# Square rows of three batches as two float32r products, one unit later, with VectorE's order refitted

## The chip, the cores and the metric

The kernel runs on 1 core of one Trainium2 chip. The metric is the device time of one execution in microseconds (us). Several runs are taken and the median is used. The engines are TensorE (PE, with its weight loads as PEld), VectorE (DVE), ScalarE (ACT), GpSimd (POOL) and SyncE (SP, which here only issues DMAs).

## What is computed

The inputs are x (4 batches of 256 channels by 512 nodes), ctx_4096 (4 batches of 1601 point dimensions by 512 nodes) and fside (4 blocks of 256 by 256 weights). Each batch has 512 nodes. Its 8 nearest neighbours are those with the smallest squared distance between columns of the points, the node itself included. Two rounds of the same four blocks follow, with one matrix for the centre and the neighbours:

```python
sq = jnp.sum(xyz * xyz, axis=1)
d2 = sq[:, :, None] + sq[:, None, :] - 2.0 * jnp.einsum('bdn,bdm->bnm', xyz, xyz)
_, idx = jax.lax.top_k(-d2, k)
...
for i in range(NUM_BLOCKS):
    shortcut = points
    p = _lrelu(points)
    g = _group_point(p, idx_t)
    c = jnp.einsum('oi,bin->bon', w_center[i], p)
    gn = jnp.einsum('oi,bikn->bokn', w_neighbor[i], g)
    points = (c + gn.sum(axis=2)) / (K + 1.0) + shortcut
```

xyz is ctx_4096, points is x, and both weights are fside. The order of distances decides the result, so the Gram products and the rest must keep float32 precision.

## The kernel before

**Products in parts.** A float32 operand is split into float32r parts: high, low and a mixed sum of both. Main products (high with high, low with low) and mixed products together give the full product. In this way TensorE works with float32r throughout. The exceptions are the square row, which is a plain float32 product, and the transposes.

**Gram stages.** For each batch b from 0 to 3, the 1601 point dimensions come in 7 units k: six of 256 dimensions and a rest of 65. For a unit, SyncE loads `raw`. ScalarE makes `g_high` (`points_high`, L522). `g_low` comes from VectorE (`points_low`, L656). For the units 1, 3 and 5 of batches 1 to 3 it comes from ScalarE, as minus high (L539), and then a GpSimd DMA that adds the source to it (L288). VectorE makes `g_mixed` (`points_mixed`, L670). TensorE does `main_products` (16 products for a unit) and `mixed_products` (8). SyncE reloads `raw` of unit k for the next batch only when TensorE has used the unit and VectorE has made its `g_mixed` (L231). All of this has in-order queues written out by hand, one list for each engine, with semaphores between them.

**Distances, one batch behind.** While TensorE does the products of batch b, the distances of batch b-1 are made. VectorE folds the two sums into `gram` (`gram_rows`, L707) and takes the diagonal, times -0.5, into `half_diag`, and its row sums into `half_sq` (`diagonals`, L716). TensorE multiplies all ones by `half_diag` (`square_row`, L377), which puts minus half the square of each column in every row of a PSUM bank. VectorE adds it up (`distances`, L723). TensorE turns the blocks that were left out (`turn_distances`, L388) and ScalarE copies them (`copy_low`, L548). VectorE finds the 8 largest of each row and marks them (`neighbours`, L731), ScalarE makes `nbr` of the marks (L557), VectorE adds the diagonal (`add_selves`, L740), SyncE turns them by DMA (`turn_neighbours`, L245) and ScalarE copies the result into `adj` (`copy_adj`, L565).

**Steps.** The 32 steps (8 layers of 4 batches) run after the Gram stages; the first enters in stage 3. For step s, ScalarE makes relu and `r_high` (L576), GpSimd `r_low` (L295), VectorE `r_mixed` (L685). TensorE makes y (`y_main`, L400, and `y_mixed`, L423). ScalarE rounds it to `y_hi` (L595). VectorE takes the rest `y_rest` (L745) and with the mixed product makes `y_lo` (L753). TensorE multiplies both by the adjacency (`out_step`, L437) in two halves, and VectorE adds them to the state (`update`, L761). In TensorE's list, `y_mixed(s)` stands between the two halves of `out_step(s - 1)`. Step 0 differs: its y_mixed stands ahead of `square_row(3)` and of the first half of `out_step(0)`.

**Lines that set the order around the change.** TensorE's list is in L457 to L515, ScalarE's in L601 to L652, VectorE's in L768 to L827 and GpSimd's in L304 to L317. In stages 1 to 3 the square row stands behind mixed_products(b, 0) in TensorE's list, at L465. In VectorE's list `distances(b - 1)` stands at L784, between low 2 and mixed 2.

Of the kernel before, what the change touches and what calls it, by code (L numbers as in the profile page):

```python
# [25 lines left out]
def knn_blocks_kernel(nc: bass.Bass, x: bass.AP, ctx_4096: bass.AP, fside: bass.AP, out: bass.AP):  # L26
# [41 lines left out]
    with es:  # L68
# [31 lines left out]
        half_diag = sb("half_diag", [P, N], fp32)  # L100
        half_sq = sb("half_sq", [P, NB], fp32)
# [97 lines left out]
        diag_ready = sem("diag_ready")  # L199
        sq_row_ready = sem("sq_row_ready")  # L200
# [86 lines left out]
        def _(pool):  # L287
# [6 lines left out]

            def relu_low(n):  # L295

                if n == 0:
                    pool.wait_ge(unit_used, (B - 1) * PAIRS + 2)
                for h in range(CH):
                    pool.wait_ge(r_high_ready, CH * n + h + 1)  # L300
                    nc.gpsimd.tensor_tensor(r_low[:, n % 3, h, :], relu[:, h, :], r_high[:, n % 3, h, :].bitcast(fp32),  # L301
                                            ALU.subtract).then_inc(r_low_ready, 1)
# [10 lines left out]
            for b in range(1, B):  # L313
                for k in BY_DMA:
                    points_low(b, k)
# [4 lines left out]
        def _(pe):  # L320
# [56 lines left out]
            def square_row(b):  # L377
# [3 lines left out]
                else:  # L381
                    pe.wait_ge(w_high_ready, BLOCKS)
                    pe.wait_ge(w_rest_ready, BLOCKS)
                pe.wait_ge(diag_ready, b * NB + NB)
                nc.tensor.matmul(bank[SQ_BANK][:, :], ones[:, :], half_diag[:, :], start=True, stop=True)\  # L385
                    .then_inc(sq_row_ready, 1)
# [70 lines left out]
            for b in range(B):  # L457
# [4 lines left out]
                else:  # L462
                    main_products(b, 1)
                    mixed_products(b, 0)
                    square_row(b - 1)  # L465
                main_products(b, 2)
                mixed_products(b, 1)
                if b > 0:
                    turn_distances(b - 1)
                main_products(b, 3)  # L470
# [47 lines left out]
        def _(act):  # L518
# [13 lines left out]

            def points_parts(b, k):

                points_high(b, k)
                if by_dma(b, k):
# [63 lines left out]

            for k in range(UNITS):  # L601
# [11 lines left out]
            for b in range(1, B):  # L613
                points_parts(b, 5)
                points_parts(b, 6)
                copy_low(b - 1)
                if b >= 2:
                    copy_adj(b - 2)
                if b == 1:
# [20 lines left out]
            for s in range(1, B * LAYERS):  # L640
# [3 lines left out]
                if s == 1:  # L644
                    copy_low(B - 1)
                    copy_adj(B - 2)
# [8 lines left out]
        def _(dve):  # L655
# [60 lines left out]
            def diagonals(b):  # L716

                for n, i in enumerate(ROWS):
# [57 lines left out]
            for b in range(1, B):  # L776
# [7 lines left out]
                distances(b - 1)  # L784
                points_mixed(b, 2)
                points_low(b, 3)
                points_low(b, 4)
                points_mixed(b, 3)
                points_low(b, 5)
                neighbours(b - 1, 0)  # L790
                neighbours(b - 1, 1)
                points_low(b, 6)
                points_mixed(b, 6)
                points_mixed(b, 4)
                neighbours(b - 1, 2)
# [12 lines left out]
            diagonals(B - 1)  # L808
            relu_mixed(1)
            y_low(0)  # L810
# [42 lines left out]
```

## Time and profile before

| what | value |
|---|---|
| time, median of 3 runs | 321.87 us (321.72 to 322.04) |
| time of the profiled execution | 321.73 us |
| its span | 319.9 us |
| TensorE busy | 314.8 us, 98% |
| VectorE busy | 251.7 us, 79% |
| ScalarE busy | 172.6 us, 54% |
| GpSimd busy | 94.0 us, 29% |
| stage 1, stage 2, stage 3 begin | 29.9, 54.4, 78.9 us |

Times in the trace count from the start of the span. The page gives each engine's busy time. The chain that ended last is followed back from the last instruction: at each step to what released it, or to the instruction before it on its engine. A timeline row gives the start, the length, the engine, the line, the operation and what it writes and reads; in square brackets stand the idle time of the engine ahead of it and what ended that. A record's length includes the time in which it waits for a port, and matmul records overlap, so TensorE's pace is read from starts or from the chain.

### The profile page before, as it was taken

The page shows a single profiled execution, that of the slowest core. Times are in us where ns is not written, and L with a number is a line of the kernel's source. Part 1 is how long each engine was busy: PE and PEld are TensorE (multiplying, and loading weights), DVE is VectorE, ACT ScalarE, POOL GpSimd, SP SyncE. Part 2 cuts the span into 40 slices and gives each one's busy share as a digit, 9 for nine tenths or more (in the row PEclk, how much of TensorE's full clock was granted, in tenths as well). Part 3 has the DMA queues.
Part 4 walks back from the last instruction along what each step waited for, and adds up shares of the span by engine and source line. Part 5 has one row for each costly group of instructions (what it writes and reads, how often), then busy time and mean ns, then how long its engine had stood idle before and what let it go on. Part 6 is the DMA issues. An engine that isn't in the chain of part 4 may idle for free.

```text
span 319.9 us, 5033 instructions
## 1 busy us (share of the span) xinstructions
PE 314.8 (98%) x1974; PEld 287.5 (90%) x1974; DVE 251.7 (79%) x333; ACT 172.6 (54%) x255; POOL 94.0 (29%) x85
## 2 busy tenths in 40 slices
PE   8999999999999899999999999999999999999996
PEld 6999999999999688898888988888888988889885
DVE  3995799899899969998777767777776767767674
ACT  4557387388377346546584455444554455544530
POOL 2011111101126304433344333443344333443330
PEclk9999999999999999999999999999999999999999
DMA  7979959988950300000300000000000000000113
GB/s 251 315 284 198 267 166 223 237 283 190 261 92 1 66 2 0 2 0 2 66 1 2 1 3 0 0 0 2 0 2 0 2 0 0 2 0 2 67 67 134
DMA packets 17313, 25.52 MB, mean 80 GB/s; under 512 B 9476, under 2 KB 10756, under 8 KB 17288
## 3 DMA queue, kind: packets, MB, share of 16 engines
q1 hardware_dynamic: 15992, 20.46, 21.3%
q0 software_dynamic: 1296, 4.72, 8.2%
q8 instruction: 16, 0.26, 0.3%
q14 instruction: 9, 0.07, 0.1%
HBM read 20.98 MB, written 2.10 MB: 72 GB/s over the span
## 4 chain that ended last, share of the span: by engine, by line
PE 96%; DVE 2%; DMA 1%; issue 0%; ACT 0%; DVEq 0%
PE wide L444 38%; PE wide L323 29%; PE wide L417 18%; PE wide L433 9%; DMA raw<-in_ctx_dram 1%; PE wide L385 1%; PE wide L392 1%; PE wide L373 1%; DVE gram L713 0%; DVE y_lo L757 0%; DVE r_mixed L690 0%; PE wide L396 0%; DVE half_diag L720 0%; ACT g_high L527 0%; DVE state L765 0%
## 5 line engine op out<-in xcount | busy, mean ns | idle before, releaser
L301 POOL TENSOR_TENSOR r_low<-relu,r_high 128x512 fp32r<-128x512 f32 x64 | 83.7, 1331 | 135.7 <-ACT r_high L593 135.7
L444 PE MATMUL wide<-adj,y_hi 128*128 128x512 f32 (+1 forms) x260 | 101.8, 393 | 1.2 <-DVE y_lo L757 1.2
L444 PE MATMUL wide<-adj,y_lo 128*128 128x512 f32 (+1 forms) x260 | 101.7, 393 | 0.0
L598 ACT CAST y_hi<-wide 128x1024 fp32r<-128x1024 f32 x32 | 32.6, 1018 | 89.2 <-PE wide L417 89.2
L750 DVE TENSOR_TENSOR y_rest<-wide,y_hi 128x1024 f32<-128x1024 f32 x32 | 39.1, 1223 | 30.3 <-ACT y_hi L598 30.2
L765 DVE SCALAR_TENSOR_TENSOR state<-wide,state 128x512 f32<-128x512 f32 (+1 forms) x65 | 44.1, 678 | 20.0 <-PE wide L444 19.9
L444 PEld LDWEIGHTS wide<-adj,y_hi 128*128 128x128 f32 x260 | 49.0, 188 | 10.7 <-issue 2.0
L444 PEld LDWEIGHTS wide<-adj,y_lo 128*128 128x128 f32 x260 | 48.9, 188 | 8.7
L593 ACT ACTIVATE r_high<-relu 128x512 fp32r<-128x512 f32 x64 | 40.6, 634 | 2.0
L590 ACT ACTIVATE relu<-state 128x512 f32<-128x512 f32 x64 | 40.2, 627 | 1.5 <-POOL r_low L301 1.5
L757 DVE SCALAR_TENSOR_TENSOR y_lo<-wide,y_rest 128x1024 fp32r<-128x1024 f32 x32 | 39.1, 1222 | 0.0
L690 DVE SCALAR_TENSOR_TENSOR r_mixed<-r_low,r_high 128x1024 fp32r<-128x1024 f32 x32 | 38.9, 1216 | 0.2 <-POOL r_low L301 0.2
L433 PEld LDWEIGHTS wide<-w_mixed,r_mixed 128*128 128x128 f32 x256 | 34.5, 188 | 2.9
L417 PEld LDWEIGHTS wide<-w_high,r_high 128*128 128x128 f32 x256 | 34.6, 188 | 2.6
L417 PE MATMUL wide<-w_low,r_low 128*128 128x256 f32 x256 | 35.5, 281 | 0.0
L417 PE MATMUL wide<-w_high,r_high 128*128 128x256 f32 x256 | 35.4, 280 | 0.0
L433 PE MATMUL wide<-w_mixed,r_mixed 128*128 128x256 f32 x256 | 35.3, 280 | 0.0
L323 PE MATMUL wide<-g_high 128*128 128x256 f32 x192 | 34.4, 322 | 0.3 <-ACT g_high L527 0.3
L530 ACT ACTIVATE g_high<-raw 128x1024 fp32r<-128x1024 f32 x23 | 23.9, 1064 | 17.5 <-DMA raw<-in_ctx_dram 17.5
L417 PEld LDWEIGHTS wide<-w_low,r_low 128*128 128x128 f32 x256 | 32.4, 188 | 0.2 <-POOL r_low L301 0.2
L323 PE MATMUL wide<-g_low 128*128 128x256 f32 x192 | 32.2, 310 | 0.0
L323 PE MATMUL wide<-g_mixed 128*128 128x256 f32 x192 | 31.5, 310 | 0.0
(57 smaller groups left out, 285.7 us busy)
## 6 DMA issues: line engine op xcount, KB each, us to landing
raw<-in_ctx_dram SPq DMA_DIRECT2D x23, 512.0 KB, 5.5
g_low<-in_ctx_dram POOLq DMA_DIRECT2D x9, 512.0 KB, 7.9
state<-in_x_dram SPq DMA_DIRECT2D x4, 512.0 KB, 8.9
out_dram<-state SPq DMA_DIRECT2D x3, 512.0 KB, 2.8
w_raw<-in_fside_BxSxS_dram SPq DMA_DIRECT2D x1, 1024.0 KB, 7.8
rest_raw<-in_ctx_dram SPq DMA_DIRECT2D x4, 130.0 KB
raw<-in_ctx_dram SPq DMA_DIRECT2D x2, 256.0 KB, 3.2
turned<-nbr SPq DMA_TRANSPOSE x16, 3.1
```

The costliest lines, as they stand in the source:

```text
L301: nc.gpsimd.tensor_tensor(r_low[:, n % 3, h, :], relu[:, h, :], r_high[:, n % 3, h, :].bitcast(fp32), ALU.subtract).then_inc(r_low_ready, 1)
L323: return nc.tensor.matmul(sums_of(i, first), part[t][:, i * P:(i + 1) * P], row_of(i, part[t]), start=(start and i < NB - 1), stop=(stop a ...
L417: mm = nc.tensor.matmul(wide[main_at(s)][:, q * C:(q + 1) * C], part[:, s % 3, h, q * P:(q + 1) * P], weights[:, w, h, :], start=(part is ...
L433: mm = nc.tensor.matmul(dst, r_mixed[:, s % 3, h, q * P:(q + 1) * P], w_mixed[:, w, h, :], start=(h == 0), stop=(h == CH - 1))
L444: mm = nc.tensor.matmul(bank[to][:, cols], part[:, s % 2, q, h * P:(h + 1) * P], adj[:, b, q, cols], start=(q == 0 and part is y_hi), stop ...
L590: nc.scalar.activation(relu[:, h, :], state[:, b, h, :], ACT.Prelu, alpha=SLOPE)\
L593: nc.scalar.mul(r_high[:, n % 3, h, :], relu[:, h, :], LEAN).then_inc(r_high_ready, 1)
L598: nc.scalar.copy(y_hi[:, s % 2, :, :], wide[main_at(s)][:, :].rearrange("p (q o) -> p q o", q=NB))\
L690: nc.vector.scalar_tensor_tensor(r_mixed[:, n % 3, :, :], r_low[:, n % 3, :, :].bitcast(fp32), -SHIFT, r_high[:, n % 3, :, :].bitcast(fp32 ...
L750: nc.vector.tensor_tensor(y_rest[:, :, :], wide[main_at(s)][:, :].rearrange("p (q o) -> p q o", q=NB), y_hi[:, s % 2, :, :].bitcast(fp32), ...
L757: nc.vector.scalar_tensor_tensor(y_lo[:, s % 2, :, :], wide[MIXED][:, :].rearrange("p (q o) -> p q o", q=NB), UNMIX, y_rest[:, :, :], op0= ...
L765: nc.vector.scalar_tensor_tensor(state[:, b, h, cols], bank[at][:, cols], SHARE, state[:, b, h, cols], op0=ALU.mult, op1=ALU.add).then_inc ...
```

## The change

The square rows of batches 0 to 2 are made of two float32r products in place of one float32 product. ScalarE rounds `half_diag` to float32r (`diag_high`), GpSimd subtracts it from `half_diag` (`diag_low`), and TensorE sums ones times each in the same bank. Batch 3's square row stays as it was. `diag_high` stands in ScalarE's list behind `points_high(b, 5)`, and `diag_low` in GpSimd's list ahead of the DMA of unit 5. TensorE's square row stands one unit later, behind `main_products(b, 2)`, and `turn_distances` behind `main_products(b, 3)`. In VectorE's list `distances` moves behind mixed 3, and low 4 and mixed 3 move ahead of it; neighbours 0 and 1 move behind the rest and mixed 4. ScalarE does `copy_adj` ahead of `copy_low`. For step 0, VectorE makes `y_lo` ahead of `r_mixed` of step 1. New waits guard the reuse of half_diag, diag_high and diag_low.

```diff
--- before.py
+++ after.py
@@ -98,6 +98,10 @@
         dist = sb("dist", [P, NB, N], fp32)
         marked = sb("marked", [P, NB, N], fp32)
         half_diag = sb("half_diag", [P, N], fp32)
+
+        diag_high = sb("diag_high", [P, N], fp32r)
+        diag_low = sb("diag_low", [P, N], fp32r)
+        ones_r = sb("ones_r", [P, P], fp32r)
         half_sq = sb("half_sq", [P, NB], fp32)
         top8 = sb("top8", [P, NB, K], fp32)
         nbr = sb("nbr", [P, NB * (N + P)], bf16)
@@ -197,6 +201,9 @@
         main_copied = sem("main_copied")
         gram_ready = sem("gram_ready")
         diag_ready = sem("diag_ready")
+        diag_high_ready = sem("diag_high_ready")
+        diag_low_ready = sem("diag_low_ready")
+        ones_r_ready = sem("ones_r_ready")
         sq_row_ready = sem("sq_row_ready")
         dist_ready = sem("dist_ready")
         low_turned = sem("low_turned")
@@ -292,6 +299,14 @@
                 pool.dma_start(g_low[k][:, :, :], src[:, 2 * k:2 * k + 2, :], accum_op=ALU.add)\
                     .then_inc(low_landed[k], 16)
 
+            def diagonal_low(b):
+
+                pool.wait_ge(diag_high_ready, b + 1)
+                if b > 0:
+                    pool.wait_ge(sq_row_ready, b)
+                nc.gpsimd.tensor_tensor(diag_low[:, :], half_diag[:, :], diag_high[:, :].bitcast(fp32), ALU.subtract)\
+                    .then_inc(diag_low_ready, 1)
+
             def relu_low(n):
 
                 if n == 0:
@@ -312,6 +327,8 @@
                                    pattern=[[-1, P]], channel_multiplier=1).then_inc(consts_ready, 1)
             for b in range(1, B):
                 for k in BY_DMA:
+                    if k == 5:
+                        diagonal_low(b - 1)
                     points_low(b, k)
             for n in range(B * LAYERS):
                 relu_low(n)
@@ -381,9 +398,18 @@
                 else:
                     pe.wait_ge(w_high_ready, BLOCKS)
                     pe.wait_ge(w_rest_ready, BLOCKS)
-                pe.wait_ge(diag_ready, b * NB + NB)
-                nc.tensor.matmul(bank[SQ_BANK][:, :], ones[:, :], half_diag[:, :], start=True, stop=True)\
-                    .then_inc(sq_row_ready, 1)
+                    pe.wait_ge(ones_r_ready, 1)
+                if b < B - 1:
+                    pe.wait_ge(diag_high_ready, b + 1)
+                    nc.tensor.matmul(bank[SQ_BANK][:, :], ones_r[:, :], diag_high[:, :], start=True, stop=False)
+                    pe.wait_ge(diag_low_ready, b + 1)
+                    nc.tensor.matmul(bank[SQ_BANK][:, :], ones_r[:, :], diag_low[:, :], start=False, stop=True)\
+                        .then_inc(sq_row_ready, 1)
+                else:
+
+                    pe.wait_ge(diag_ready, b * NB + NB)
+                    nc.tensor.matmul(bank[SQ_BANK][:, :], ones[:, :], half_diag[:, :], start=True, stop=True)\
+                        .then_inc(sq_row_ready, 1)
 
             def turn_distances(b):
 
@@ -462,12 +488,13 @@
                 else:
                     main_products(b, 1)
                     mixed_products(b, 0)
+                main_products(b, 2)
+                if b > 0:
                     square_row(b - 1)
-                main_products(b, 2)
                 mixed_products(b, 1)
+                main_products(b, 3)
                 if b > 0:
                     turn_distances(b - 1)
-                main_products(b, 3)
                 mixed_products(b, 2)
                 if b == 0:
                     pe.wait_ge(consts_ready, 2 + NB)
@@ -530,9 +557,20 @@
                     nc.scalar.mul(unit(k, g_high, rest_high), unit(k, raw, rest_raw), LEAN / ROOT)\
                         .then_inc(g_high_ready[k], 1)
 
+            def diagonal_high(b):
+
+                if b > 0:
+                    act.wait_ge(sq_row_ready, b)
+                    act.wait_ge(diag_low_ready, b)
+                act.wait_ge(diag_ready, b * NB + NB)
+                nc.scalar.copy(diag_high[:, :], half_diag[:, :]).then_inc(diag_high_ready, 1)
+
             def points_parts(b, k):
 
                 points_high(b, k)
+                if b > 0 and k == 5:
+
+                    diagonal_high(b - 1)
                 if by_dma(b, k):
 
                     act.wait_ge(g_high_ready[k], parts_up_to(b, k))
@@ -598,6 +636,8 @@
                 nc.scalar.copy(y_hi[:, s % 2, :, :], wide[main_at(s)][:, :].rearrange("p (q o) -> p q o", q=NB))\
                     .then_inc(y_hi_ready, 1)
 
+            act.wait_ge(consts_ready, 1)
+            nc.scalar.copy(ones_r[:, :], ones[:, :]).then_inc(ones_r_ready, 1)
             for k in range(UNITS):
                 points_high(0, k)
             points_parts(1, 0)
@@ -613,9 +653,9 @@
             for b in range(1, B):
                 points_parts(b, 5)
                 points_parts(b, 6)
-                copy_low(b - 1)
                 if b >= 2:
                     copy_adj(b - 2)
+                copy_low(b - 1)
                 if b == 1:
                     for l in range(BLOCKS):
                         act.wait_ge(w_rest_ready, l + 1)
@@ -642,8 +682,8 @@
                 if 3 <= s + 1 <= LAST_STEP:
                     relu_parts(s + 1)
                 if s == 1:
+                    copy_adj(B - 2)
                     copy_low(B - 1)
-                    copy_adj(B - 2)
                 if s == 4:
                     neighbour_marks(B - 1, 0)
                 if s == 6:
@@ -715,6 +755,8 @@
 
             def diagonals(b):
 
+                if b > 0:
+                    dve.wait_ge(diag_low_ready, b)
                 for n, i in enumerate(ROWS):
                     dve.wait_ge(gram_ready, b * NB + n + 1)
                     nc.vector.scalar_tensor_tensor(half_diag[:, i * P:(i + 1) * P], gram[:, i, i * P:(i + 1) * P], -0.5,
@@ -781,17 +823,15 @@
                 points_low(b, 1)
                 points_mixed(b, 1)
                 points_low(b, 2)
-                distances(b - 1)
                 points_mixed(b, 2)
-                points_low(b, 3)
                 points_low(b, 4)
                 points_mixed(b, 3)
-                points_low(b, 5)
-                neighbours(b - 1, 0)
-                neighbours(b - 1, 1)
+                distances(b - 1)
                 points_low(b, 6)
                 points_mixed(b, 6)
                 points_mixed(b, 4)
+                neighbours(b - 1, 0)
+                neighbours(b - 1, 1)
                 neighbours(b - 1, 2)
                 neighbours(b - 1, 3)
                 points_mixed(b, 5)
@@ -806,8 +846,8 @@
             y_remainder(0)
             gram_rows(B - 1)
             diagonals(B - 1)
+            y_low(0)
             relu_mixed(1)
-            y_low(0)
             for s in range(1, B * LAYERS):
                 y_remainder(s)
                 if s == 1:
```

## Rows read from the trace of the kernel before

**Rows 1.** The page: span, and each engine's busy time, share and instructions.

```profile
span 319.9 us, 5033 instructions
...
PE 314.8 (98%) x1974; PEld 287.5 (90%) x1974; DVE 251.7 (79%) x333; ACT 172.6 (54%) x255; POOL 94.0 (29%) x85
```

**Rows 2.** Timeline of VectorE, end of stage 2 and start of stage 3.

```profile
74.77 1.22 DVE L681 SCALAR_TENSOR_TENSOR g_mixed<-g_low,g_high 128x1024 fp32r<-128x1024 f32 x1
...
82.28 1.22 DVE L681 SCALAR_TENSOR_TENSOR g_mixed<-g_low,g_high 128x1024 fp32r<-128x1024 f32 x1
83.42 1.22 DVE L666 SCALAR_TENSOR_TENSOR g_low<-g_high,raw 128x1024 fp32r<-128x1024 f32 x1
85.86 1.93 DVE L727 SCALAR_TENSOR_TENSOR dist<-wide,half_sq,gram 128x384 f32<-128x384 f32 x4 [1.23 <-PE wide L385]
```

**Rows 3.** The chain that ended last, in order: start us, us, what.

```profile
60.45 0.86 PE wide L385 x2
61.31 3.53 PE wide L323 x24
...
110.49 0.14 issue
110.62 2.11 PE wide L444 x8
...
113.67 1.88 PE wide L444 x8
...
122.79 2.11 PE wide L417 x16
...
129.60 1.88 PE wide L417 x16
```

**Rows 4.** Timeline of VectorE around step 0.

```profile
108.12 1.22 DVE L690 SCALAR_TENSOR_TENSOR r_mixed<-r_low,r_high 128x1024 fp32r<-128x1024 f32 x1
109.26 1.21 DVE L757 SCALAR_TENSOR_TENSOR y_lo<-wide,y_rest 128x1024 fp32r<-128x1024 f32 x1
...
116.42 0.68 DVE L765 SCALAR_TENSOR_TENSOR state<-wide,state 128x512 f32<-128x512 f32 x1
```

**Rows 5.** Timeline of TensorE: square row of stage 3, and step 0.

```profile
84.80 1.02 PE L385 MATMUL wide<-half_diag,ones 128*128 128x512 f32 x2
...
107.17 1.10 PE L433 MATMUL wide<-w_mixed,r_mixed 128*128 128x256 f32 x8
108.35 1.10 PE L385 MATMUL wide<-half_diag,ones 128*128 128x512 f32 x2
```

**Rows 6.** Timeline of ScalarE: the first pass, and unit 5 of batches 1 to 3.

```profile
3.75 0.63 ACT L527 ACTIVATE g_high<-raw 128x512 fp32r<-128x512 f32 x1 [1.73 <-DMA raw<-in_ctx_dram]
...
31.89 1.06 ACT L530 ACTIVATE g_high<-raw 128x1024 fp32r<-128x1024 f32 x1 [2.30 <-DMA raw<-in_ctx_dram]
...
56.43 1.07 ACT L530 ACTIVATE g_high<-raw 128x1024 fp32r<-128x1024 f32 x1 [1.83 <-DMA raw<-in_ctx_dram]
...
84.45 1.06 ACT L530 ACTIVATE g_high<-raw 128x1024 fp32r<-128x1024 f32 x1 [4.49 <-DMA raw<-in_ctx_dram]
```

**Rows 7.** Timeline of GpSimd, the first three r_low.

```profile
94.05 1.75 POOL L301 TENSOR_TENSOR r_low<-relu,r_high 128x512 fp32r<-128x512 f32 x1 [6.29 <-ACT r_high L593]
95.76 2.88 POOL L301 TENSOR_TENSOR r_low<-relu,r_high 128x512 fp32r<-128x512 f32 x1
98.60 1.29 POOL L301 TENSOR_TENSOR r_low<-relu,r_high 128x512 fp32r<-128x512 f32 x1
```

**Rows 8.** Timeline of VectorE in the same stretch.

```profile
93.97 0.68 DVE L666 SCALAR_TENSOR_TENSOR rest_low<-rest_high,rest_raw 65x512 fp32r<-65x512 f32 x1
94.68 1.67 DVE L681 SCALAR_TENSOR_TENSOR rest_mixed<-rest_low,rest_high 65x512 fp32r<-65x512 f32 x1
96.28 1.21 DVE L681 SCALAR_TENSOR_TENSOR g_mixed<-g_low,g_high 128x1024 fp32r<-128x1024 f32 x1
```

**Rows 9.** DMA issues open at 76.06: KB each, us to landing; unit 5.

```profile
raw<-in_ctx_dram SPq DMA_DIRECT2D x1, 512.0 KB, 8.4
```

## The prediction

> **What bounds the kernel now.** I read the page's busy shares first, then the chain that ended last in order of time, then the timelines of the five queues around each square row and around step 0. TensorE is busy 98% of the span [rows 1] and the chain is its products almost throughout, so whatever shortens TensorE's own row of work counts in full, and whatever makes it wait counts in full too. TensorE works at its full granted clock in all 40 slices of the page. VectorE, 79% busy on average, is no spare engine in the three Gram stages (stage 1 to 3: batch b's products, with batch b-1's distances inside): it waits only once in a stage, 1.23 us for the square row [rows 2]. The one place where TensorE itself waits long is step 0: some 1.2 us between the square row of batch 3 and the first adjacency product, for y_lo (109.45, worked out below, to 110.62 [rows 3]). In the chain that is VectorE's r_mixed of step 1 and then y_lo, with 0.14 behind it [rows 3, 4].
>
> **The square row itself.** Its float32 product stands in the chain with 0.86 us. A float32r product of 512 columns is there one eighth of 1.88, that is 0.235, and two are 0.47 [rows 3]. Each of three square rows gains 0.39, together 1.17 us, all of it on TensorE's path. Their weight load is one of 128 columns as in front of every product and adds nothing seen. The row moves behind main_products(b, 2), 16 products or 2.35 us later at 3.53 for 24 [rows 3]. The record of stage 3's row begins at 84.80 [rows 5]; two earlier gains of 0.39 and the move put it at 84.80 - 0.78 + 2.35 = 86.37, and its second product, which needs diag_low, at 86.60. By the same sum stage 2 wants diag_low near 62.5 and stage 1 near 38.5.
>
> **What must now be ready.** A copy by ScalarE (diag_high), then a subtraction by GpSimd (diag_low). ScalarE's copy stands behind points_high(b, 5), which waits for the raw DMA. A 128x512 pass of ScalarE is 0.63, one of 128x1024 1.06 [rows 6]. GpSimd's subtraction has the shape of r_low: 1.29 undisturbed [rows 7]. From landing to diag_low that is 1.06 + 0.63 + 1.29, near 3.0 us, plus what GpSimd waits.
>
> **What GpSimd waits for.** Three records of r_low show it, against VectorE's records beside them [rows 7, 8]. The first took 1.75 instead of 1.29: it got going at 94.51, while VectorE's rest_low (93.97, 0.68) was ending and its successor rest_mixed depended on it, so nothing of VectorE's was queued; rest_mixed in turn took 1.67. The second, asked for at 95.76, took 2.88: not only rest_mixed but also the g_mixed behind it, which started at 96.28 and was not slowed (1.21), went ahead, and GpSimd began about 97.35, 1.07 after g_mixed started. The MAX8 behind g_mixed, with one input in SBUF, held nobody up. I read: two-input VectorE operations that follow each other without a dependence keep GpSimd out for all of them; a dependent pair lets it in between. One instance speaks for the first half, so I keep the other reading as a rival.
>
> The new order of VectorE puts mixed 1, low 2, mixed 2, low 4, mixed 3 in a row, all with two inputs in SBUF, and only then distances. Steps of 1.14 [rows 2]; the single dependent pair is low 2 and mixed 2.
> - Stage 1: raw 5 is there at 31.89 [rows 6], GpSimd asks near 33.5 and gets in as low 2 ends, 34.5. diag_low is ready at 35.8, wanted at 38.5. No cost.
> - Stage 2: raw 5 is there at 56.4 [rows 6], but the diagonals end only at 57.8 (24.5 before the 82.28 of [rows 2]); GpSimd asks at 58.5, gets in at 60.0, is ready at 61.3, wanted at 62.5. No cost on TensorE; mixed 2 is held 1.2 us. The wait of 1.23 for the square row is gone, so VectorE is level with before: mixed 5 again starts near 74.77, and stage 3's mixed 1 near 82.25 [rows 2].
> - Stage 3: SyncE issues raw 5 of batch 3 only after mixed 5 of batch 2 (about 76.0, as before). It took 8.4 to land [rows 9], hence the 84.45 of ScalarE [rows 6]. Then high to 85.5, diag_high to 86.1, and GpSimd asks when mixed 2 is running or done. VectorE: 82.25, low 2 at 83.39, mixed 2 at 84.64, low 4 at 85.78, mixed 3 at 86.92. By my reading GpSimd starts 1.07 into mixed 3, at 88.0, and is ready at 89.3. **TensorE waits 2.7 us** from 86.60. An earlier landing doesn't help unless it comes by 82.9, in time for low 2's end at 84.5.
>
> The Trainium skill states on this, in SBUF — State Buffer, section "SBUF: two separate sides", that VectorE and GpSimd share a port pair as an exclusive lock and that the one that starts first has it for its whole instruction. The rows agree with the lock; that a waiting GpSimd is passed over a second time (the 2.88) goes beyond the page. By its rule the wait would be what the rival below has.
>
> **What else moves, and its cover.** Behind diag_high ScalarE does low 5's preparation 0.6 later and behind diag_low GpSimd issues that DMA 0.6 to 2.5 later; TensorE wants it over 10 us after that issue. copy_low comes about 2 us later, since the turned distances do (two products blocks more ahead of them), and copy_adj now goes ahead of it from stage 2 on: the transposes had landed before 66.2 and 90.7, where it began without a wait. This makes copy_low(1) about 1 us late, and VectorE reaches neighbours 0 at 69.0, after it. copy_main of stage 1 slips by 1.3 and ends just before stage 2's fourth product wants it. mixed 5 of batch 2 is ready at 75.9 and wanted at 76.4 (the 84.80 of [rows 5] less 5.89 for the stage so far, less 1.77, less 0.78). No cost, but half a microsecond of cover; if it goes, each tenth is paid. ones_r is a 128-column copy at 2 us, under the first load. In stage 3, SyncE's loads are past. Unseen are the accumulation with a satisfied wait in its middle (0 to 0.05 each, I take 0; a gain has no source).
>
> **Step 0.** y_lo needs the mixed products, over at 107.17 + 1.10 = 108.27 [rows 5], and the engine free after the diagonals at 108.12 [rows 4]. It starts at 108.30 instead of 109.26: 0.96 less wait, with TensorE's square row over at 109.45 just ahead [rows 5]. r_mixed of step 1, now behind it, is ready at 110.65, wanted at 111.6. Next, VectorE's chain up to state (0, 1) stays where it is, 116.42 + 0.68 = 117.10 [rows 4], and the adjacency products of step 1 would want it at 117.0: 0.1 to 0.2 comes back. The 2.11 of y_main(3) against 1.88 elsewhere [rows 3] is a wait for r_low; copy_adj(2) ahead of copy_low(3) frees ScalarE earlier, so some 0.2 goes. Sum: 1.0, bounds 0.8 and 1.2. These times ride on the end of the Gram sums, so they hold whether stage 3 is early or late.
>
> **Sum.** -1.17 - 1.0 + 2.7 = +0.5 us. The profiled execution took 321.73 (span 319.9 and 1.8 around it), 0.14 under the median of 321.87; against the median the sum gives 322.4. About 0.2%, 0.64 us, is what a measurement can tell here from no change.
>
> **Rivals.**
> - *The port is handed over at each instruction's end.* GpSimd asks at 86.1 in low 4, gets in at 86.86, is ready at 88.15: TensorE waits 1.55, the sum is -0.6 and the time 321.2. If raw 5 lands 1 us earlier it gets in at 85.7, waits 0.4, and 320.1 results. For it: a lock given in turn is the plain reading, and it also explains the first and second r_low up to 96.28. Against it: g_mixed not slowed at 96.28. 17%.
> - *No wait at all.* Raw 5 lands by 82.9, or VectorE is 1.5 later than I have it, so that low 2's end comes after the request. Raw 4 of that batch is now issued 1.5 us earlier, into a gap of the DMA queues, which speaks for an earlier landing; 1.5 us at once is much. 319.7. 21%.
> - *Slower: GpSimd is not let in between low 2 and mixed 2 either* (the place: all three stages; it decides if that gap, 0.03 us, is too short). Then diag_low comes 1.07 + 1.29 after mixed 3's start: stage 1 ready at 39.3, wait 0.75; stage 2 at 64.75, wait 2.25; stage 3, with TensorE 3.0 later and VectorE tied to its Gram sums 1.35 later, 1.1. In all 4.1 - 2.2 = +1.9: 323.8. Against it stands the 1.75 record. 12%.
> - *As forecast*: 322.4, by itself 321.7 to 323.1. 50%.
>
> **How the numbers follow.** From 319.5, under the case without a wait, to 323.4, short of the centre of the slower one. Faster by over 0.2%: all of the no-wait case, and most of the first rival, 0.36. Within: two thirds of the forecast and the rest of the first rival, 0.36. Slower: the other third, and the slower rival, 0.28.
>
> **What the profile would show.** L385's successors: two products 0.235 apart in the chain instead of 0.86; no TensorE idle before them in stages 1 and 2, and some 2.7 in stage 3, released by GpSimd's diag_low, whose record there is near 3 us long and ends after VectorE's mixed 3. In stages 1 and 2 diag_low's record is 2.3 to 2.8 long and mixed 2's over 2.3. y_lo of step 0 at about 0.03 behind the mixed products, and TensorE's 1.2 down to 0.2. Wrong would be: diag_low of stage 3 beginning inside the row of five; a TensorE wait for g_mixed, main_copied or low_copied in stage 2 or 3; or a fall of the granted clock behind the 2.7 us, twice the longest idle time after the start that this trace has.

## The result, and the profile after

The changed kernel took 324.85 us in the median of four executions (323.55 to 325.53) against 321.87 before (four executions, 321.72 to 322.04), a ratio of 1.0072 (95% interval 1.0044 to 1.0099). The forecast was 322.4 with a range of 319.5 to 323.4, so it was wrong. Medians and ranges here count all executions of a kernel, ratios leave out those more than 1.5% above its fastest. Measured again, on two chips, with 12 executions each, the same kernel had medians of 322.08 (ratio 0.9992, 0.9972 to 1.0012) and 322.13 (0.9993, 0.9965 to 1.0021). The 24 times go from 320.53 to 325.82; seven are below 321.5, four above 324. The kernel before, executed 152 times beside all experiments (one execution of over 1000 us left out), has a median of 322.21, and five above 324. So, over many executions, the change leaves the median where it was; it moves the low end of the times down and widens their upper end. The rest of this document takes these two effects apart. That the medians of 24 executions lie 0.3 us from the forecast is luck; the part on the prediction says why.

The page of the changed kernel, and TensorE's timeline. Rows with rest_mixed are the last of a batch's products, 0.59 before the next stage.

```profile
span 321.7 us, 5048 instructions
...
PE 316.3 (98%) x1974; PEld 288.6 (90%) x1974; DVE 255.4 (79%) x333; ACT 173.9 (54%) x259; POOL 97.0 (30%) x88
```

```profile
31.14 0.76 PE L340 MATMUL wide<-rest_mixed 65*128 65x256 f32 x4
...
40.00 0.40 PE L404 MATMUL wide<-diag_high,ones_r 128*128 128x512 f32 x1
40.24 0.40 PE L406 MATMUL wide<-diag_low,ones_r 128*128 128x512 f32 x1
...
55.28 0.76 PE L340 MATMUL wide<-rest_mixed 65*128 65x256 f32 x4
...
79.90 0.76 PE L340 MATMUL wide<-rest_mixed 65*128 65x256 f32 x4
...
87.94 1.45 PE L340 MATMUL wide<-g_low 128*128 128x256 f32 x8 [0.20 <-DVE g_low L706]
89.22 0.39 PE L404 MATMUL wide<-diag_high,ones_r 128*128 128x512 f32 x1
...
109.45 1.20 PE L459 MATMUL wide<-w_mixed,r_mixed 128*128 128x256 f32 x8 [0.32 <-DVE gram L753]
111.21 1.10 PE L411 MATMUL wide<-half_diag,ones 128*128 128x512 f32 x2 [0.56 <-DVE half_diag L762]
```

Before, the three rest_mixed rows stood at 29.29, 53.80 and 78.31. The span is 1.8 us shorter before (319.9 against 321.7), and 1.85 of that are there when stage 1 begins, ahead of every square row. Stage 1 is 24.14 long instead of 24.51: the gain of the two products is there, 0.37 of 0.39. Stage 2 is 24.62, so it is lost again. From the start of stage 3 to the end it takes 241.2 us, before 241.0, where the sum without a wait for diag_low had 1.4 less. The square row of stage 3 finds diag_low ready, against my forecast; what waits is g_low 2. At step 0, TensorE waits twice for VectorE's Gram sums and diagonals, which [rows 5] did not have.

VectorE, ScalarE and GpSimd in stage 3 show why:

```profile
85.56 2.32 DVE L706 SCALAR_TENSOR_TENSOR g_low<-g_high,raw 128x1024 fp32r<-128x1024 f32 x1
...
96.88 0.69 DVE L778 MAX8 top<-dist 128x8 f32<-128x512 f32 x1 [1.18 <-ACT dist L589]
```

```profile
85.32 1.48 POOL L307 TENSOR_TENSOR diag_low<-half_diag,diag_high 128x512 fp32r<-128x512 f32 x1 [5.35 <-ACT diag_high L566]
```

```profile
83.46 1.06 ACT L557 ACTIVATE g_high<-raw 128x1024 fp32r<-128x1024 f32 x1 [1.46 <-DMA raw<-in_ctx_dram]
...
94.69 2.00 ACT L606 CAST adj<-turned 128x1024 fp32r<-128x1024 bf16 x2 [7.98 <-DMA turned<-nbr]
96.59 0.26 ACT L589 COPY dist<-wide 128x128 f32<-128x128 f32 x1
97.43 0.66 ACT L628 ACTIVATE relu<-state 128x512 f32<-128x512 f32 x1
```

ScalarE sits 8 us on copy_adj, for the transposes of batch 1. copy_low behind it is late by 2.4 (TensorE's transposes end at 94.2), VectorE waits 1.18 for it, and relu of step 0 begins at 97.43. The DMA view has the last transpose of that group at 7.7 us to landing; the kernel before had 3.7:

```profile
turned<-nbr SPq DMA_TRANSPOSE x1, 7.7
```

```profile
turned<-nbr SPq DMA_TRANSPOSE x1, 3.7
```

### The profile page after: what moved, and what is told of

Same layout as the page of the kernel before. It is cut to its first block, busy times and chain, and to the rows that moved or that the text cites. A ratio compares the mean times of both kernels' runs of the same rounds, so it can differ in the third digit from the quotient of the medians.

```text
span 321.7 us, 5048 instructions
## 1 busy us (share of the span) xinstructions
PE 316.3 (98%) x1974; PEld 288.6 (90%) x1974; DVE 255.4 (79%) x333; ACT 173.9 (54%) x259; POOL 97.0 (30%) x88
## 4 chain that ended last, share of the span: by engine, by line
PE 83%; DVE 5%; ACT 5%; DMA 3%; SPq 2%; issue 1%; DVEq 1%
PE wide L470 37%; PE wide L443 18%; PE wide L340 17%; PE wide L459 9%; DMA turned<-nbr 2%; SPq L258 2%; ACT g_high L557 1%; DVE g_mixed L721 1%; DVE g_low L706 1%; DMA raw<-in_ctx_dram 1%; DVE gram L753 1%; DVE marked L780 1%; ACT g_low L577 1%; ACT w_low L662 1%; ACT adj L606 1%
## 5 line engine op out<-in xcount | busy, mean ns | idle before, releaser
L316 POOL TENSOR_TENSOR r_low<-relu,r_high 128x512 fp32r<-128x512 f32 x64 | 82.4, 1309 | 138.8 <-ACT r_high L631 127.5
L730 DVE SCALAR_TENSOR_TENSOR r_mixed<-r_low,r_high 128x1024 fp32r<-128x1024 f32 x32 | 40.0, 1250 | 0.0
L340 PE MATMUL wide<-g_high 128*128 128x256 f32 x192 | 33.4, 317 | 0.5 <-ACT g_high L554 0.5
L340 PE MATMUL wide<-g_low 128*128 128x256 f32 x192 | 33.4, 317 | 0.3 <-DVE g_low L706 0.2
```

Source lines behind the costliest of these rows:

```text
L340: return nc.tensor.matmul(sums_of(i, first), part[t][:, i * P:(i + 1) * P], row_of(i, part[t]), start=(start and i < NB - 1), stop=(stop a ...
L730: nc.vector.scalar_tensor_tensor(r_mixed[:, n % 3, :, :], r_low[:, n % 3, :, :].bitcast(fp32), -SHIFT, r_high[:, n % 3, :, :].bitcast(fp32 ...
```

## The experiments

Eighteen runs, two of them of the changed kernel as it is (e1, e12) and two of one other kernel (e10, e16). Each was executed five to twelve times, between executions of the kernel before on the same chip. Ratios are to those. The medians of the kernel before were 321.96 to 322.31 from one set of executions to the next, so medians of two sets differ by some 0.3 us without a cause.

**The change again (e1, e12).** No edit.

> The changed kernel again, unaltered, for the spread of its times and a second profile. In the first profile stage 1 began at 31.74 where before had 29.88, 1.86 us late, all of it from raw loads of batch 0 and 1 that landed later (ScalarE's pass of batch 1, unit 0: 21.70 against 19.04). Theory A (chance of the DMAs): the second profile shows another start of stage 1, somewhere between 29.9 and 32, and the times scatter by 1 to 2 us while the kernel before keeps within 0.4. Theory B (the change itself makes the first loads late): stage 1 begins at 31.5 to 32 in every profile, and the median stays at 324.5 to 325.

322.08 (320.69 to 325.73). Its profiled execution took 320.94: stages 1 and 2 of 24.15 and 24.63, last transpose 3.7, copy_adj at 89.43, TensorE idle 0.26 at step 0. Stage 1 begins at 30.20. So the 1.85 of the first profile does not come each time. From stage 3 to the end it takes 240.0 us, 1.2 less than the first profile of the same kernel, where the last transpose took 7.7.

> The changed kernel once more, unaltered, beside the three above on the same chip. Four executions had a median of 324.85, twelve others one of 322.08. Both theories: again between 321.5 and 325 with a scatter of 3 us or more; in its profile the last transpose of stage 3 takes over 6 us if unit 5's DMA is issued among the transposes, and under 4 if it isn't.

322.13 (320.53 to 325.82). In its profile unit 5's DMA was issued at 86.08, the last transpose at 86.7, and that took 6.7. As expected. Stage 1 begins at 31.50.

**y_lo of step 0 alone (e2).**

```diff
             diagonals(B - 1)
-            relu_mixed(1)
             y_low(0)
+            relu_mixed(1)
```

> The kernel before with y_lo of step 0 ahead of r_mixed of step 1, nothing else. If my sum for this part holds it gains 0.8 to 1.2 us (320.7 to 321.1), TensorE starts the first adjacency product at about 109.65 instead of 110.62. The rival: something else is late next, r_mixed or the state, and the gain is under 0.3 us.

321.44, ratio 0.9979 (0.9961 to 0.9997), 0.75 below before. The profile has the product at 109.62, and y_main of step 4 at 128.44 instead of 129.44, with 0.06 of that from an earlier start of stage 1: 0.94. My sum for this part stands.

**Tensors and copy of ones (e3, e17, e18).** e3 is the kernel before with the three tensors laid out and the copy; e17 has the moved addresses alone, e18 the copy alone.

```diff
+        diag_high = sb("diag_high", [P, N], fp32r)
+        diag_low = sb("diag_low", [P, N], fp32r)
+        ones_r = sb("ones_r", [P, P], fp32r)
...
+            act.wait_ge(consts_ready, 1)
+            nc.scalar.copy(ones_r[:, :], ones[:, :]).then_inc(ones_r_ready, 1)
```

> The kernel before with the three new tensors laid out in SBUF where the change has them and the copy of ones to ones_r on ScalarE, with its wait on TensorE; all else as before, the square rows in float32. Theory B of the late first loads (the moved addresses or the copy do it): stage 1 begins near 31.7 and the time is 323.5 to 324. Theory A: stage 1 begins near 29.9 and the time is 321.6 to 322.2.

322.33 (321.28 to 327.72), ratio 1.0016 (0.9984 to 1.0049). The profiled start of stage 1 is 30.2, as theory A has it; but five of 12 times are above 324.

> The kernel before with the three new tensors laid out where the change has them, so that half_sq and all behind it lie 4.5 KB further in every partition, and nothing else. If moved addresses slow the loads of stage 0: some 4 of 12 times above 324, as with tensors and copy together (321.28 to 327.72). If it is the copy, or chance: as before, 321.5 to 323.5, and one at most above.

322.31 (321.57 to 323.62), ratio 1.0001 (0.9986 to 1.0016): none above 324.

> The kernel before with the copy of ones to ones_r and its wait, with ones_r as the last tensor, so that nothing else moves. If the copy slows the start: some 4 of 12 above 324. If neither this nor the moved tensors alone has more than one above 324, the five high times were chance or take both.

322.53 (321.62 to 327.96), ratio 1.0016 (0.9985 to 1.0047): three above 325. In the kernel before, 8 of 24 executions with the copy are above 324, and 5 of 152 without it. The median hardly moves. No execution above 324 of these was profiled, so how a 0.30 us copy at 2.03 us does it stays open. Two things speak against the copy alone. None of the 48 executions of e5, e9, e10, e15 and e16 below, which all have the copy, is above 324 (one of 514.91 left out), and e8, which has no copy, has 11 of 12 above it. And it need not be the start: in the profiles of e3 and e18 stage 1 begins at 30.2, and in e3's the last transpose of stage 3 took 6.2, as in the changed kernel.

**copy_low first (e4).**

```diff
-                if b >= 2:
-                    copy_adj(b - 2)
                 copy_low(b - 1)
+                if b >= 2:
+                    copy_adj(b - 2)
```

> The changed kernel with copy_low(b-1) ahead of copy_adj(b-2) in ScalarE's list again, as the kernel before has it in stages 2 and 3. In the first profile of the changed kernel ScalarE sat 7.0 and 8.0 us before copy_adj on the transposes, copy_low of stage 3 came at 96.59 with its transposes over at 94.2, VectorE waited 1.18 for it and was late at the last Gram sums, where TensorE waits some 1.7. Theory (the order costs): 0.8 to 1.5 us faster than the changed kernel. Rival (other waits fill in at once): within 0.3 us of it.

323.82, ratio 1.0031 (1.0002 to 1.0061): slower, a miss for both theories. Six of 12 are above 324. In its profile, of an execution of 325.44, the last transpose takes 11.3; copy_low is in time, but copy_adj begins at 97.15 and relu of step 0 stands behind it all the same. So the order of the two isn't the cause. The late transposes are what ScalarE waits for here; whether they are the cause is tested below.

**State loads behind the transposes (e5, e6).** SyncE, in the changed kernel and in the one before:

```diff
-                load_state(b - 1)
-            load_state(B - 1)
-            for b in range(1, B):
+                if b < B - 1:
+                    load_state(b - 1)
+            turn_neighbours(1)
+            load_state(B - 2)
+            load_state(B - 1)
+            for b in range(2, B):
                 turn_neighbours(b)
```

> The changed kernel; only SyncE's loads of state 2 and 3 (1 MB) stand behind the transposes of batch 1's neighbours instead of ahead of them. Theory M: what makes the changed kernel slow and scattered is that the last transpose of stage 3 lands late in a full DMA (89.4 in the fast profile, 94.7 and 97.2 in the slow ones), so copy_adj(1), copy_low(2), relu and the last Gram sums are late. Then this one has the transposes landed by 88, TensorE waits under 0.5 in all from 86 to 116, the median falls to 320.5 to 321.2 and the scatter to about 1 us. Theory R (GpSimd's diag_low holding VectorE's g_low 2 is the cost): no change, median 322 to 324.

321.17 (320.47 to 323.95), ratio 0.9967 (0.9942 to 0.9992). The last transpose took 2.9 in the profile. The median is theory M's; the rest of what I gave for it is not: the transposes landed at 90.3, TensorE waited 0.64 and 0.27 from 86 to 116, and the times scatter by 3.5.

> The kernel before with the same move of the two state loads. Theory M: before has its transposes in by 89.4 to 90.6 in all profiles, just in time, so the move gives it 0 to 0.4 in the median, mostly by a smaller scatter. If the gain of the move is as large here as in the changed kernel (over 1 us), the transposes aren't what the change made worse.

321.93, ratio 0.9977 (0.9957 to 0.9996). The two measures differ. By the medians the kernel before gains 0.4 from the move and the changed one 0.9 (322.08 or 322.13 to 321.17). By the ratios it is 0.7 and 0.8 (1 to 0.9977, and 0.9992 to 0.9967). So this pair doesn't show that the change made the transposes worse; only the guard below does. (The profiled execution of e5 was its slowest, 323.95: stage 1 began at 31.2 and TensorE waited 1.24 in stage 2 for mixed 5, the cover of half a microsecond that I had named.)

**diag_low on VectorE (e7).** One tensor_tensor behind g_low 2, none on GpSimd.

> The changed kernel with diag_low made by VectorE behind g_low 2, instead of by GpSimd. Theory R: g_low 2 takes 1.22 again instead of 2.32, TensorE's gaps of 0.26 and 0.37 before g_low 2 in stages 2 and 3 go, stages 2 and 3 are 0.3 to 0.4 shorter each, and the median is 0.6 to 0.8 better than the changed kernel's. Theory M: those gaps go as well, but the transposes still land late in many executions, and the scatter of 320.7 to 325.7 stays.

323.06 (320.01 to 325.45), ratio 0.998 (0.9945 to 1.0015). Both sides of the expectation for theory M hold: the gaps in stages 1 to 3 go (24.15 and 24.14), the best time is 0.5 better than the changed kernel's best, and the scatter stays. The median missed the 0.6 to 0.8 of theory R: four of 12 are above 324. The transposes took 7.4 to 13.1 in its profile, of an execution of 325.09. There copy_adj begins at 96.17, and TensorE waits 2.27 for the first r_high; the granted clock is then 0.50, that is 1.2 GHz, for the 3 us behind the wait, where it is 1.00 in the kernel before. The record of 8 products takes 2.05 there, against 1.10 to 1.21:

```profile
101.56 2.05 PE L433 MATMUL wide<-w_high,r_high 128*128 128x256 f32 x8 [2.27 <-ACT r_high L621]
```

```profile
core 0: us, PE busy (x) PEld busy (x) DVE busy (x) ACT busy (x) POOL busy (x), PEclk, DMA share, GB/s
101.50:104.50 3.00, 2.94 (x14) 2.97 (x15) 2.85 (x7) 2.94 (x5) 2.24 (x3) 0.50 0.01 3
```

I had named such a fall as a sign of being wrong, for another wait. No other profile has it, but the mean granted clock of an execution is 0.989 to 0.995 in eight of e8's twelve, in two of e3's and in three of e18's, all above 325. What TensorE waited for in those isn't known.

**The order alone (e8), and the guard.** e8 has the changed order on all queues, with float32 square rows.

> The order of the changed kernel on all queues (square row and turned distances one unit later, distances behind mixed 3, copy_adj ahead of copy_low, y_lo of step 0 first), but the square rows in float32 as before, without diag_high and diag_low. Theory M: it is as slow and as scattered as the changed kernel or more (322 to 324), since copy_low is 2 to 2.4 us later and the GpSimd DMAs of units 1 and 3 behind it are too. Theory R: without the two extra operations it is at 321 to 321.5 with the scatter of the kernel before.

328.55 (322.88 to 329.55), ratio 1.0076 (1.0035 to 1.0118). The ratio counts only five of the twelve executions, of median 324.97. The slowest kernel of all has neither diag_high nor diag_low. That is theory M's side, though its 322 to 324 was far too low. Its profile is of its fastest execution and has the last transpose at 8.0; its executions near 329 have no profile.

At this point ten profiles of stage 3 could be laid side by side. Times of the GpSimd DMA of unit 5 and of the last transpose, and how long this took:

| kernel | unit 5 issued | last transpose issued | it took |
|---|---|---|---|
| before | 86.9 | 85.7 | 3.7 |
| e1 | 87.3 | 85.7 | 3.7 |
| e2 | 85.7 | 84.5 | 3.7 |
| e6 | 87.2 | 84.3 | 2.5 |
| e5 | 88.1 | 87.4 | 2.9 |
| e4 | 86.1 | 85.9 | 11.3 |
| first profile after | 86.7 | 87.0 | 7.7 |
| e3 | 83.7 | 84.6 | 6.2 |
| e7 | 83.9 | 84.8 | 11.4 |
| e8 | 84.9 | 86.0 | 8.0 |

Where the accumulating DMA comes 0.7 us or more behind the last transpose, that takes under 4; where it comes among them or within 0.3 behind, 6.2 to 11.4. The other ten profiles, taken later, agree: 3.7 in eight, 6.7 and 6.3 in e12 and e15, where the DMA is ahead of the last transpose. Stage 2 shows the same in the transposes of batch 0: 5.9 to 8.8 in the eight profiles where unit 5's DMA is ahead of the last transpose, 3.1 to 4.7 in the ten where it comes 0.8 or more behind. The kernel before is one of the eight (58.88 against 59.96, 5.9): its transposes still land at 65.9, and its copy_adj begins at 66.16 without a wait.

A table of profiles only shows that the two go together. The guard, one wait of GpSimd's queue ahead of unit 5's DMA until the transposes of the group before have landed, tests it by force, in the changed kernel (e9), with VectorE's diag_low (e10) and in the order alone (e11, whose lines these are):

```diff
             for b in range(1, B):
                 for k in BY_DMA:
+                    if b >= 2 and k == 5:
+                        pool.wait_ge(nbr_turned, 16 * NB * (b - 1))
                     points_low(b, k)
```

> The order of the changed kernel with float32 square rows (median 328.55 without the guard), with the same guard on the DMA of unit 5. Theory C: the median falls by 6 us or more, to 321.3 to 322.3. Rival S: it stays above 325.

321.25, ratio 0.9976 (0.995 to 1.0001): by one wait, 7.3 us off the median of all executions, or 3.2 by the ratios (1.0076 to 0.9976). One execution of 12 is above 324, against 11. In its profile: last transpose 3.7, copy_adj at 88.57, TensorE's idle time at step 0 0.24.

> The changed kernel; GpSimd issues the accumulating DMA of unit 5 of batches 2 and 3 only when the transposes of batch 0's and 1's neighbours have landed. In ten profiles of stage 3 the last transpose took 2.5 to 3.7 us where that DMA was issued 0.7 us or more behind the last transpose, and 6 to 13 where it was issued among the four or within 0.2 of the last. Theory C (this collision is what scatters and slows the changed kernel): last transposes land within 4 us, copy_adj(1) starts at 88 to 91 in the profile, the median is 320.3 to 321.2 and nothing is above 323. Rival S (the DMA is simply full there, whoever is in it): the transposes still take 6 to 12, median 322 to 323.

321.49 (320.45 to 322.75), ratio 0.9977 (0.996 to 0.9993). Nothing is above 323 and the last transpose took 3.7, as theory C has it, but the median is higher than I gave: 0.6 below that of e12 on the same chip, with intervals that overlap. What the guard takes from the changed kernel for sure is the high times. Its profile shows the stall that I had forecast for the change, at a third of the size, because raw 5 landed at 86.18:

```profile
88.36 0.40 PE L406 MATMUL wide<-diag_high,ones_r 128*128 128x512 f32 x1
89.65 0.50 PE L408 MATMUL wide<-diag_low,ones_r 128*128 128x512 f32 x1 [0.90 <-POOL diag_low L307]
```

> As the run before with diag_low by VectorE as well. The best time of that version alone was 320.01, its median 323.06 with scatter to 325.45, its profiled transposes 8 to 13 us. Theory C: median 319.9 to 320.5, 0.4 to 0.8 better than with diag_low on GpSimd, since g_low 2 isn't held. Rival S: as scattered as before, median 322.5 to 323.5.

320.25 in eight executions; seven go from 319.59 to 321.73, and one of 514.91 us, at a mean granted clock of 0.56, stands alone. The ratio is 0.9935 (0.9912 to 0.9959). Theory C. The same order with the same guard and float32 square rows is e11, executed on the same chip: 321.25. The 1.0 us between them is the three square rows, of which the stages show 0.37 each.

**What the parts are worth (e13 to e16).** e14 is the kernel before with the guard, e13 adds y_lo first, e16 is e10 again.

> The kernel before with the guard alone: the DMA of unit 5 of batches 2 and 3 waits for the transposes. In its profiles that DMA was issued 1.2 to 2.9 us behind the last transpose anyway, so if only the change brings the collision about, the median stays within 0.3 us of before and only the highest times (323 to 325) go. If before suffers from it in most executions too, it gains 0.7 us or more.

322.39, ratio 1.0015 (1.0 to 1.003). Nothing gained, and 0.4 more than the median of the kernel before, a little over the 0.3 that I gave: before doesn't suffer from the collision, and the guard may cost it something.

> The kernel before with y_lo of step 0 first and the guard. If the gains add up: 320.9 to 321.3, the 0.95 of step 0 below the run with the guard alone. What the guarded version with VectorE's diag_low has beyond it (320.25 so far) is the square rows, 0.6 to 1.1 us of the 1.17 worked out.

321.14 in 11 executions, ratio 0.998 (0.997 to 0.999). e11, which has the new order besides, is at 0.9976: with the guard, the order costs nothing that can be seen.

> The changed kernel with diag_low by VectorE and the guard, once more: 320.0 to 320.5, 1.8 to 2.2 us below before, with a scatter under 2.5.

320.02 (319.58 to 320.55, five executions), ratio 0.9942 (0.993 to 0.9954). 1.9 below before, and 1.1 below e13, which lacks the square rows and the new order. Its TensorE rows, with the stages at 24.14 each:

```profile
29.48 0.76 PE L332 MATMUL wide<-rest_mixed 65*128 65x256 f32 x4
...
53.62 0.76 PE L332 MATMUL wide<-rest_mixed 65*128 65x256 f32 x4
...
77.76 0.76 PE L332 MATMUL wide<-rest_mixed 65*128 65x256 f32 x4
```

Last, why does unit 5's DMA fall among the transposes in the changed kernel? e15 holds raw 5 of batch 3 back until unit 3 is prepared.

```diff
                     sp.wait_ge(g_mixed_ready[k], b)
+                    if b == B - 1 and k == 5:
+                        sp.wait_ge(minus_high_ready[3], b)
```

> The changed kernel; in batch 3 SyncE issues raw 5 only when unit 3's minus high is ready, so unit 3's accumulating DMA goes out just ahead of raw 5, as in the kernel before, and not behind it. In the profiles raw 5 took 7.2 to 8.7 us to land where unit 3's DMA was ahead of it or within 0.4, 4.3 to 6.5 where it came 0.9 or more behind. If that order is the link: raw 5 takes 7 us or more, unit 5's DMA is issued at 87.5 or later, behind all four transposes, the last transpose takes under 4, copy_adj(1) starts by 91.5; the cost goes to diag_low, for which TensorE waits 1 to 2 us in stage 3; the median is 321.5 to 322.5 and scatters less. If the order is no link: raw 5 takes about 5, and the transposes 6 to 11 as before.

321.1 (320.35 to 323.62), ratio 0.9985 (0.9968 to 1.0001). The median is 1.0 better than the changed kernel's, the ratio 0.2 (0.9985 against 0.9992), and not by my mechanism: unit 3's DMA still went out behind raw 5, by 0.2, raw 5 took 4.3, and unit 5's DMA (84.6) still came ahead of the last transpose (85.1, 6.3). Other profiles speak against the link too: raw 5 took 4.8 in e3, with unit 3's DMA 0.45 ahead of it, and 5.3 and 4.9 in e10 and e12, with it 0.3 to 0.4 behind. So why raw 5, and with it unit 5's DMA, comes early stays open.

## Why the prediction was wrong, step by step

In the first profile three things stand against the sum, and the sum had none of them: the start (1.85 us), g_low 2 (0.48 in stage 2, a wait of 0.20 in stage 3) and the late transposes (1.2, against the profile of e1). The 2.7 us that it did have never came.

- **Square rows, 0.39 each: right.** Two products 0.24 apart. Stages 1 and 2 are 0.37 shorter in each profile where nothing else interferes (e7, e10, e16: 24.14 or 24.15 against 24.51), and the three are worth 1.0 in the medians (e11 against e10).
- **Step 0, 1.0: right where the Gram sums are in time.** 0.94 in e2's profile, 0.75 in its median. Where they are late, as in the first profile after, it goes.
- **The 2.7 us for diag_low in stage 3: wrong.** The step that failed is "two-input VectorE operations that follow each other without a dependence keep GpSimd out for all of them". The 21 diag_low records of seven profiles take 1.37 to 2.27, never the wait of a second operation: GpSimd gets the port at the end of the VectorE instruction that holds it. That was my first rival, and it is what the Trainium skill states in SBUF — State Buffer, section "SBUF: two separate sides". VectorE's next operation then takes 2.2 to 2.33, whether or not it depends on the one before. The page's rule leaves the second r_low of [rows 7] open: it was passed over for g_mixed, and it is no accident of one execution, since it takes 2.87 or 2.88 in all eight profiles with the old order (before, e2, e3, e6, e13, e14, e17, e18). What sets it apart is that it follows another GpSimd operation at once; nothing run here tests that. I made a rule of the one place where it happens. When raw 5 is late the stall exists, 0.90 in e9.
- **Stage 2, "No cost on TensorE; mixed 2 is held 1.2 us": wrong, a term put at nothing.** The held one is g_low 2, as in stage 3 above, and TensorE wants it at once. Stage 2 is 24.62 to 24.64 in five of the seven profiles with GpSimd's diag_low (first after, e1, e4, e9, e15) and 24.14 or 24.15 with VectorE's: 0.48, more than the stage's square row gains. In e12, where diag_low held g_mixed instead (2.21), it is 24.52; e5's 26.10 has the wait of 1.24 in it.
- **The cover of copy_adj: the step whose failure the guard shows.** I wrote that the transposes "had landed before 66.2 and 90.7" and took that over. It holds only while unit 5's DMA stays behind them. I had noted that this DMA moves, and asked only whether TensorE would get its data in time, not what it would run into. In the first profile copy_adj begins at 94.69, after a wait of 7.98, and that costs 1.2 us, the whole of step 0's gain and more; in the order alone the guard against it is worth 3.2 us by the ratios and 7.3 in the medians.
- **The start: not seen.** It is the largest piece of the first profile: 1.85 us lie before anything that the sum touched. The raw load of batch 1, unit 0, lands 2.7 us later there (21.7 against 19.0). In eleven other profiles with the copy of ones, stage 1 begins between 29.7 and 31.5, in eight without it (before, e2, e6, e8, e11, e13, e14, e17) between 29.7 and 30.4. Late starts of 31.2 to 31.7 are in four profiles, all of the changed kernel or of it with one wait or load moved (first after, e5, e9, e12), and not in those of e3 and e18. What brings them is not shown. That the copy raises the number of executions above 324 in the kernel before is shown by the counts of e3 and e18; the way is not, and in the 48 executions of the other kernels with the copy that are named there it raises nothing.

Without the 2.7 the sum gives 319.7. The kernel with neither the held g_low 2 nor the late transposes comes near it: 320.25 (e10) and 320.02 (e16). In the changed kernel as it is, these two and the wider scatter take back what the parts gain, so that the medians of 24 executions, 322.1, lie beside the forecast of 322.4. That is luck: one cost that doesn't exist stood in for others that I had put at nothing. Why all four of the first measurement lay above 323.5 is not settled: only the fastest of them has a profile. The range was too narrow because it held only the waits of the sum, and no scatter of the DMAs, though the first loads and the raw passes all end on a DMA.

## What to carry to other kernels

When a step is moved, follow its DMA to the transfers that it will now stand beside, and not only to its own consumer; a transfer that was in time by a microsecond in one profile is a bet. Here a queue guard of one wait was worth more than the operations that the change was about. Give a changed kernel in a full DMA at least a dozen executions before its median is believed.

## What the runs showed of the hardware that I had not expected

- In stage 3 the last transposing DMA of a group took 2.5 to 3.7 us in the 13 profiles where the accumulating DMA of 512 KB came 0.7 us or more behind it, and 6.2 to 11.4 in the seven where it came earlier. Another of e7's group took 13.1. Raw loads of unit 5 in the same stretch took 4.3 to 8.7.
- Port sharing goes by single instructions: VectorE's 1.22 became 2.32 beside a GpSimd subtraction of 1.29, and GpSimd waited at most 1.0 in 21 records. The second r_low of the kernel before, 2.88 in place of 1.29, is the exception.
- A ScalarE copy of 128x128 at the very start, put into the kernel before, went with 8 executions of 24 above 324 us, against 5 of 152.
- Behind 2.27 us in which TensorE waited, its granted clock was 0.50 (e7, 101.5 to 104.5 us); the waits of up to 1.24 that the other profiles have after the first 20 us had no such fall behind them.
